# Differential attention layer: turning normalised tokens without TensorE, and 27 more exp blocks on VectorE

## What is computed

```python
h = _layernorm(x) * (1 + ca) + sa
q, k = einsum(h, Wq), einsum(h, Wk)          # 32 half-heads of 8 features; v: 16 heads of 16
attn_w = softmax(q @ k.T * hd ** -0.5)       # 2048 x 2048 for each half-head and batch
aw = attn_w[:, :, 0] - lam * attn_w[:, :, 1]
attn = rms_norm(aw @ v) * subln_w * (1 - LAMBDA_INIT)
x = x + ga * (attn @ Wo.T)
h = _layernorm(x) * (1 + cb) + sb
x = x + gb * (h @ (ternary(weight) * scale).T)
```

## Time and profile before

| | |
|---|---|
| median of 3 runs | 3611.5 us (3609.34 to 3612.31) |
| profiled execution | 3607.35 us, span 3605.5 us |
| granted TensorE clock, mean | 0.998 |
| PE busy | 3405.9 us, 94% |
| ScalarE busy | 3534.4 us, 98% |
| VectorE busy | 2588.9 us, 72% |
| GpSimd busy | 338.0 us, 9% |
| DMA | 136.90 MB, mean 38 GB/s |

### The profile page before, as it was taken

One profiled execution on the slowest core, in us unless ns is written; L12 is line 12 of the kernel. 1 busy time (PEld: TensorE's weight loads), 2 busy tenths in 40 slices (PEclk: granted clock), 3 DMA queues, 4 the chain that ended last, 5 costly groups with the idle time before them and its releaser, 6 DMA issues. The chain is left out here.

```text
span 3605.5 us, 76890 instructions
## 1 busy us (share of the span) xinstructions
PE 3405.9 (94%) x32302; PEld 799.1 (22%) x32302; DVE 2588.9 (72%) x3808; ACT 3534.4 (98%) x2808; POOL 338.0 (9%) x229
## 2 busy tenths in 40 slices
PE   8999999999899999999999999999999999989998
PEld 5222112122122222222222222222221222211222
DVE  6687878863578687776367768677547888878886
ACT  5999999999999999999999999999999999999998
POOL 3010101010010100101001010100100000000001
PEclk9999999999999999999999999999999999999999
DMA  6111110111101111101111001111012110010000
GB/s 196 28 32 39 32 31 22 35 39 33 38 21 42 48 35 40 50 23 33 36 47 50 25 31 36 40 49 36 20 31 63 45 37 22 17 30 16 20 22 26
DMA packets 103700, 136.90 MB, mean 38 GB/s; under 512 B 9916, under 2 KB 88716, under 8 KB 103340
## 3 DMA queue, kind: packets, MB, share of 16 engines
q1 hardware_dynamic: 102524, 131.01, 12.9%
q10 hardware_dynamic: 816, 0.79, 0.1%
HBM read 72.50 MB, written 59.19 MB: 37 GB/s over the span
## 5 line engine op out<-in xcount | busy, mean ns | idle before, releaser
L1146 ACT ACTIVATE probs<-ps 128x1536 f32<-128x1536 f32 (+1 forms) x2732 | 3497.4, 1670 | 15.5 <-PE ps L1263 13.9
L1291 PE MATMUL ps<-probs,values 128*32 128x512 f32 x14600 | 2047.9, 606 | 4.9 <-DVE wmod_sb L1644 2.4
L1263 PE MATMUL ps<-queries,keys 25*128 25x512 f16 x7680 | 1003.9, 385 | 160.6 <-ACT probs L1146 142.0
L1263 PEld LDWEIGHTS ps<-queries,keys 25*128 25x128 f16 x7680 | 249.8, 91 | 1947.3 <-ACT probs L1146 1861.5
L1291 PEld LDWEIGHTS ps<-probs,values 128*32 128x32 f32 x14600 | 300.2, 108 | 416.9 <-issue 410.5
L1623 DVE TENSOR_SCALAR d_y<-ps 128x512 f32<-128x512 f32 x240 | 165.6, 690 | 295.4 <-PE ps L1263 284.7
L1708 DVE STREAM_TRANSPOSE seg_t<-ps 128x512 f32<-128x512 f32 x127 | 91.0, 716 | 356.9 <-PE ps L1291 356.4
L1060 POOL TENSOR_TENSOR seg_rs<-seg_ms,neg_half 128x16 f32<-128x16 f32 x64 | 185.7, 2901 | 1506.1 <-DVE seg_ms L1721 1506.1
L1640 DVE SCALAR_TENSOR_TENSOR wmod_sb<-wmod_sb 128x1024 f32<-128x1024 f32 x204 | 249.6, 1224 | 6.3
L1644 DVE SCALAR_TENSOR_TENSOR wmod_sb<-wmod_sb,gates 128x1024 f32<-128x1024 f32 x204 | 249.5, 1223 | 6.0
L1642 DVE SCALAR_TENSOR_TENSOR wmod_sb<-wmod_sb,d_y 128x1024 f32<-128x1024 f32 x204 | 249.3, 1222 | 5.3
(11 more groups left out here) (181 smaller groups left out, 1690.9 us busy)
## 6 DMA issues: line engine op xcount, KB each, us to landing
v_scr<-a_v SPq DMA_DIRECT2D x16, 1024.0 KB, 5.6
values<-v_scr SPq DMA_DIRECT2D x29, 512.0 KB
queries<-q_scr SPq DMA_DIRECT2D x116, 96.0 KB
keys<-k_scr SPq DMA_DIRECT2D x116, 96.0 KB
e_x<-in_x_dram SPq DMA_DIRECT2D x18, 512.0 KB, 5.2
attn_scr<-seg_o SPq DMA_DIRECT2D x254, 32.0 KB
e_attn<-attn_scr SPq DMA_DIRECT2D x31, 256.0 KB, 3.6
out_dram<-e_y SPq DMA_DIRECT2D x15, 512.0 KB, 3.3
```

The costliest lines, as they stand in the source:

```text
L1146: nc.scalar.activation(probs[:, s % PRING, at, :], ps[:, base + at.start:base + at.stop:at.step, :], ACT.Exp, scale=1.0 / SQUARE).then_inc ...
L1263: last = nc.tensor.matmul(ps[:, score_bank(n), :], keys[buf][at, u * P:(u + 1) * P], queries[buf][at, tc * CH:(tc + 1) * CH], start=True, ...
L1291: last = nc.tensor.matmul(pv[row:row + VW, :], values[buf][:, n % SEG_BANKS // HEADS, j // 2, :], probs_of(n), start=(i == 0), stop=(i == ...
```

## The change

1. *Turning.* The transposes of `normed` leave PE, except for the first batch's prologue and the last 512 tokens. `norm_apply` writes `normed` ordered by squares; VectorE transposes the 32x32 squares in place of their grid (`turn_normed`, 1024 elements); SyncE moves the squares to their rows with 16 DMAs of 32 KB (`turn_squares`); GpSimd applies scale and shift (`scale_turned`, two instructions of 512 elements) and signals `a_evacuated` or `e_evacuated`. There are 27 turns: 12 of a-jobs and 15 of e-jobs. Steps 0 and 1 of a, 2 and 3 of e disappear from the schedule.
2. *Blocks.* `shared` gives two blocks to nearly every segment, 231 in all, at units 3 and 5, 8 and 10, with heads sought by `heads_of`; each block has its own scratch (`g_y`, `g_n`). `share_read` multiplies to 2^23 log2(e) and writes int32; whole and fractional part come out by bit operations, and three passes of polynomial and one product remain.
3. *Exp bias.* ScalarE's exp gets an immediate bias ln 8, to match the blocks' polynomial, which is scaled.
4. *Steps spread.* In the bodies of batches 1 and 2, except the last of each, the pieces stand every 2.8 units from unit 16 on.
5. *Short sums.* `segment_sums` is four entries: transpose and reciprocal at their place, the rest as filling work due three slots later. Norm statistics are due by slots after what they need, and GpSimd's order (`pool_order_of`) has its own clock and no wait for blocks.
6. In the prologue the first a-job's norm moves behind the gate weights.

```diff
-    D_UNITS = ((4, 6), (8, 10))
+    D_UNITS = ((3, 5), (8, 10))
     def shared(k):
...
-        return 2 if sum(light.get(step, 3) for step in steps) <= 5 and not normed else 1
+        return 2
...
+        if 0 < b < B - 1 and not turn:
+            spread = [[NB + 14 * (PIECES * j + p) // 5 for p in range(PIECES)] for j in range(A_MADE + len(E_MADE))]
+            put("a", body + NC, [(), ()] + spread[0:4] + spread[6:8])
+            put("e", body - GP, spread[4:6] + [(), ()] + spread[8:10])
...
+            if entry[0] == "sums":
+                later.extend((entry[2] + SUMS_AT, 0, SUMS_COST[part], ("rest", entry[1], part)) for part in range(1, sums_parts(entry[1])))
+            elif entry[0] in ("a_apply", "e_apply"):
+                later.append((slot_at(clock) + APPLY_AT, 0, 1600, ("turn", entry[0], entry[1])))
...
+            def turn_squares(kind, job):
+                sp.wait_ge(square_turned, TURN_OF[kind, job] + 1)
+                for row in range(P // 32):
+                    for col in range(P // 32):
+                        src = turned[32 * col:32 * col + 32, :, 32 * row:32 * row + 32]
+                        dst = hT[32 * row:32 * row + 32, :, :].rearrange("p c (n t) -> p (c n) t", n=BPC)[:, :, 32 * col:32 * col + 32]
+                        sp.dma_start(dst, src).then_inc(turn_done, DMA)
...
+            def scale_turned(kind, job, c):
+                if c == 0:
+                    pool.wait_ge(turn_done, (TURN_OF[kind, job] + 1) * SQUARES * DMA)
+                nc.gpsimd.tensor_scalar(hT[:, c, :], hT[:, c, :], cols_sb[:, first + 1, c, m:m + 1], cols_sb[:, first, c, m:m + 1], ALU.mult, ALU.add).then_inc(done, 1)
...
-                        if shares:
-                            pool.wait_ge(d_done, shares)
...
-                nc.scalar.activation(probs[:, s % PRING, at, :], ps[:, base + at.start:base + at.stop:at.step, :], ACT.Exp, scale=1.0 / SQUARE).then_inc(exp_done, 1)
+                nc.scalar.activation(probs[:, s % PRING, at, :], ps[:, base + at.start:base + at.stop:at.step, :], ACT.Exp, bias=EIGHT, scale=1.0 / SQUARE).then_inc(exp_done, 1)
...
-                            if i == 0 and p == 0:
-                                pe.wait_ge(a_normed, job + 1)
-                            elif i == 2 and p == 0:
+                            if i == A_FIRST_MADE and p == 0:
                                 pe.wait_ge(a_evacuated, (job - NC) * A_STEPS + 2)
...
+            def turn_normed(applied, job):
+                dve.wait_ge(a_normed if applied == "a_apply" else e_normed, job + 1)
+                dve.wait_ge(turn_done, TURN_OF[applied[0], job] * SQUARES * DMA)
+                V.transpose(turned[:, :, :].rearrange("p n f -> p (n f)"), normed[:, :, :].rearrange("p n e -> p (n e)")).then_inc(square_turned, 1)
...
                 if part == 0:
-                    link.then(V.tensor_scalar(d_n, y, ROUND, -ROUND, ALU.add, ALU.add))
+                    link.then(V.tensor_scalar(whole.bitcast(I32), f.bitcast(I32), WHOLE_BITS, WHOLE_FLIP, ALU.bitwise_and, ALU.bitwise_xor))
                 elif part == 1:
-                    link.then(V.scalar_tensor_tensor(d_y[:, :], d_n, SHIFT, y, ALU.subtract, ALU.subtract))
+                    link.then(V.tensor_scalar(f.bitcast(I32), f.bitcast(I32), PART_BITS, PART_SIGN, ALU.bitwise_and, ALU.bitwise_or))
                 elif part == 2:
-                    link.then(V.tensor_scalar(d_n.bitcast(mybir.dt.int32), d_n, BIAS, 2.0 ** 25, ALU.add, ALU.mult))
+                    link.then(V.scalar_tensor_tensor(f, f, POLY[0], f, ALU.add, ALU.mult))
```

More of the change, by code:

```diff
@@ L297, in schedule @@
                 opens = queue[0][0] == "m" or queue[0][3] == 0
-                if opens and s < closed + (NORMED if queue[0][0] == "e" and queue[0][2] == 2 else APART) and not last:
+                if opens and s < closed + APART and not last:
                     break
@@ L414, in order_of, with pool_order_of, first_of, take @@
         if b < B - 1:
-            order.append(("sums", (b + 1) * GP * SEGS - 1))
-        return order
+            k = (b + 1) * GP * SEGS - 1
+            order.append((clock, "sums", k, 0))
+            order.extend((clock, "rest", k, part) for part in range(1, sums_parts(k)))
+        return order
+    TURN_WAIT = 12000
+    def pool_order_of(b):
+        order, scales, held, clock = [], [], [], 0
+        def first_of(until):
+            heads = [queue for queue in (scales, held) if queue and max(clock, queue[0][0]) < until]
+            return min(heads, key=lambda queue: max(clock, queue[0][0])) if heads else None
+        def take(queue):
+            nonlocal clock
+            ready, cost, task = queue.pop(0)
+            order.append(task)
+            clock = max(clock, ready) + cost
+        for at, what, *task in order_of(b):
+            while first_of(at):
+                take(first_of(at))
+            if what == "turn":
+                scales.extend((at + TURN_WAIT, 800, ("scale", task[0][0], task[1], c)) for c in range(EC))
+            elif what in ("a_stats", "e_stats") or what == "rest" and task[1] == 3:
+                order.append((what, *task))
+                clock = max(clock, at) + (2900 if what == "rest" else 1010)
+            elif what == "evacuate" and task[0] == "a" and 2 <= task[2] < 6:
+                held.append((at, 1900, ("split", task[1], task[2] - 2)))
+        while first_of(STARTS[-1] + 10 ** 9):
+            take(first_of(STARTS[-1] + 10 ** 9))
+        return order
+    TURNS = [("a", NC)]
+    for body in range(B * GP):
+        for _, kind, job, i, p in sorted((u, *step) for u, step in steps_of(body).items()):
+            if kind == "e" and i == 1 and p == PIECES - 1:
+                TURNS.append(("e", job))
+        if body + 1 < (B - 1) * GP:
+            TURNS.append(("a", body + 1 + NC))
+    TURN_OF = {turn: n for n, turn in enumerate(TURNS)}
     LAST_JOB = (B - 1) * NC
@@ L1056, in _ @@
                         e_power(task[0])
-                    elif what == "sums" and (task[0] % 2 and task[0] < ALL_SEGS - 1 or task[0] == ALL_SEGS - 2):
+                    elif what == "rest":
                         rows = slice(0, P if task[0] % 2 else 64)
@@ L1897, in _ @@
                         a_apply(task[0])
+                    elif what == "turn":
+                        turn_normed(*task)
                     elif what == "gates":
```

258 lines of the change are left out of this document (135 added, 123 removed).

## The result

| | before | after |
|---|---|---|
| median | 3609.8 us (3608.48 to 3612.31, 6 runs) | 3596.8 us (3591.95 to 3600.04, 6 runs) |
| profiled execution | 3607.35 us, span 3605.5 | 3599.45 us, span 3597.6 |
| first exp | 76.1 us | 78.5 us |

The ratio is 0.996, 95% interval 0.9951 to 0.997: the change gains 13 us. The forecast was 3590, a gain of 21.5 on the median of 3611.5 known then; the time lies in its range of 3576 to 3608, and at the upper edge of its likeliest part, 3582 to 3597.

A forecast was written before the change was run, and what follows sets the result against it. ScalarE's exp stream was taken as the bound. Terms -22.7 - 4 - 6 + 9 + 2 = -21.7 took the profiled 3607.35 us to 3585.7, and the median, with its offset, to 3590; range 3576 to 3608.

The forecast's parts named there:

- Part 1, the slots: 27 more VectorE blocks turn 54 ScalarE exps from wide to narrow at 0.42 us each: -22.7 us.
- Part 2, PE's relief: Transposes leaving PE free 82 us of its work, little of it on the path: -4 us.
- Part 3, the turns hidden: The new chain VectorE, SyncE's DMAs, GpSimd's scales takes 13 to 16 us per turn and stays hidden: 0.
- Rival (c): Turns come late and PE's in-order queue holds scores and exps: +43 us at 24 us per turn, 3633; chance 0.07.
- Part 4, short sums: With only the reciprocal ahead of a segment's first read, stalls at twelve segment starts go: -6 us.
- Part 4, collisions: At seven places VectorE's evacuation, stats and the sums' rest between two reads delay scores by 1 to 1.7 us each: +9.
- the seven places: Spots where two VectorE reads stand around an evacuation, stats and the sums' rest, taking 5.6 us against three exps' 3.6.
- Part 5: GpSimd's splits and scales now run beside VectorE and lengthen its work, mostly off the path: +2 us.
- Bias 0 ns: The immediate bias in ScalarE's exps was taken to cost nothing: 0.
- contention: VectorE slowed by about 0.57 us per us of GpSimd, counting only just ahead of a read: +2 us.

The follow-up runs named there:

- e6: The changed kernel with the block pattern of the kernel before (27 segments have one block instead of two, 204 in all): 3617.6 us, ratio 1.0021 to the kernel before.
- e1: The changed kernel run again unaltered, beside the kernel before on the same chip: 3595.5 us, ratio 0.9958.
- e11: The kernel before with the changed kernel's 231 blocks, the rest of it kept: 3631.3 us, ratio 1.0057.
- e9: The changed kernel with each turn's 16 square DMAs cut in two (32 of 16 KB): 3678.9 us, ratio 1.0185 to the kernel before.
- e4: The kernel before with each segment's first block read at units 3 and 5 instead of 4 and 6: 3714.1 us, ratio 1.028.
- e7: The changed kernel with the rest of each segment's sums due at once, ahead of the first read: 3737.3 us, ratio 1.0352 to the kernel before.
- e3: The changed kernel with bounds and gates not allowed to run over VectorE's next due work: 3589.6 us, ratio 0.9938 to the kernel before.
- e5: The changed kernel with exp bias 0 instead of the immediate 2.079: 3598.9 us, ratio 0.9968 to the kernel before.
- e10: The changed kernel with the second pass of each of GpSimd's 48 splits done twice: 3598.1 us, ratio 0.9964 to the kernel before.
- e2: The changed kernel with reads in the first segments of batches 1 to 3 moved to units 5, 7, 9, 11: 3582.6 us, ratio 0.9924 to the kernel before.
- e8: The changed kernel with later first reads in batches 1 to 3, and bounds and gates kept off due work: 3575.3 us, ratio 0.9906 to the kernel before.

## Why the prediction was right, and where it was off

The sign, the range and the main mechanism, cheaper slots, were right; the account of what else the change costs was not, and errors in it partly cancelled. Of the 21.7 us forecast on the profiled execution, 7.9 came in the first trace of after and 12.8 in the second (spans 3605.5, 3597.6, 3592.7). The second balances so: slots -22.0, batch starts +4.9, other stalls at single places -1.1, first exp +2.9, many small delays +2.8, tail -0.4.

- **Part 1, the slots: right.** Two stretches of one piece each give the price. Before:

```profile
1983.64 733.75 ACT L1146 ACTIVATE probs<-ps 128x1536 f32<-128x1536 f32 x570 [0.15 <-PE ps L1263]
...
L1146 ACT ACTIVATE probs<-ps 128x1536 f32<-128x1536 f32 x494 | 692.7, 1759 | 0.3 <-PE ps L1263 0.2
L1146 ACT ACTIVATE probs<-ps 128x1024 f32<-128x1024 f32 x76 | 100.0, 1316 | 0.0
```

  After, the piece at 1051.09 above has 496 wide and 100 narrow in 758.61 us. The difference, 24.9 us for 2 wide and 24 narrow, gives 0.926 a narrow one with wide ones taken at 1.333: 0.407 per exp, 22.0 us for 54, where 22.7 was forecast. The medians of the distances between starts in the trace of after, 1.331 and 0.925, say the same. The bit passes took 0.69 as taken, VectorE's sum fell to 2566 (forecast 2550 to 2620), and e6 finds the 22 us again.
- **Part 2, PE's relief: not settled.** I took -4, and +2 for GpSimd beside VectorE. Nothing undid the relief alone, and no gain of this kind shows: delays of under 0.25 us between exps, where I had looked for it, add up to 13 us before and 16 in e1. PE's busy time fell by 49 us, not 82. In e11, with transposes on PE and 27 blocks more on VectorE, PE's queue waits for `normed` up to 4.7 us, 11.9 in three waits; so the relief's worth may depend on the blocks.
- **Part 3, the turns hidden: right, with luck.** The sum for a turn was 13 to 16 us; measured are 15.1 to 21.9 (issue 0.65 to 0.76 each, 11.72 for 16 in the turn shown under e9, not 0.46; scales 1.2 each on the mean, not 0.68). At the two tightest places the turn took 17.4 us, and I had the product 15 us behind its start: by my own cover it would have come 2.4 us late twice. It stood 17.8 behind and came 0.3 us behind the scale. Rival (c) took 43 us for turns of 24; no run has such turns, but e9's, of 25 to 31, cost 83, so its 43 was probably too low. Missing from it was the queue on GpSimd, which I had costed at nothing because the planner puts the scale 12 us behind the turn. That holds until a turn is late.
- **Part 4, short sums: here a term is missing, the move of the first reads.** "Twelve segment starts have a full sums entry ahead of a read. With reciprocal alone ahead of it I take -6": those stalls went for the most part (the piece of after that begins at 1051.09 runs through segment 36; away from the batch starts PE's waits for `d_y` fell from 6.2 us in 13 to 1.5 in 5, and waits for `g_y`, 3.1 us in 7, are new), but I priced the short sums against reads at unit 4 and did not price the move of all first reads to unit 3, which the diff holds. Without short sums the move costs the kernel before 103 us (e4), and leaving the short sums out of the changed kernel costs 141 (e7). With them it still costs the cover at three batch starts, 5 to 8 us more than before, and a good part of the missing gain went there. The row of before that should have warned is the one of d_y in the earlier trace rows (9.7 us of VectorE's idle time ended by "issue", in three waits): I left it out of the sum as small.
- **Part 4, collisions: +9 was too much.** Five of the seven places cost under 0.3 us and two about 0.5. From the first read to the second it took 3.5 to 4.8 us there, not 5.6. So the sign that I had named, waits of 1 to 1.7 us at these seven places and none elsewhere, did not come: the long waits for reads stood at the batch starts. What cost instead were the bounds ahead of seg_t at two other places, 5.9 us (e3), where I hadn't looked since no read stands between.
- **Part 5: right.** Bias 0 ns (e5), contention +2 taken and at most a few us found (e10, which adds to the splits alone); 0.33 us of VectorE per us of GpSimd in e10, not 0.57.

So the sum held by errors that partly cancel, which is luck: collisions 7 to 8 us too dear; not seen, 11 to 14 of batch starts and late transposes, 3 of a later first exp, and some 5 of small delays (3 more where 2 fewer were forecast). Together with the slots' 0.7 too little, and some 2 us more of the old stalls gone than forecast, these make, within their roundings, the 9 us by which the second trace missed the forecast; in the medians it is 7 (3597 against 3590).

What stays open: whether the prologue of after is later by itself (up to 2.5 us), what VectorE's pause at a batch's start is, and why it lasts 3.2 to 4.1 us in most traces and 5.7 and 5.8 at batch 1 in two (e7, after). A change in which the pause was removed, not covered, wasn't tried. Nor was the changed kernel with all its reads left at units 4 and 6: whether the move to 3 and 5 brings anything is not known.

## What to carry to other kernels

Price a moved instruction against what stands ahead of it in its new place, and parts of a change that lean on each other together: here 27 more blocks alone lose 20 us, reads one unit earlier alone 103, and the change without its short sums 141. A loss list grouped by place (where does the bound engine's timeline break?) found some 20 us in five places that the totals hid, and two small edits took it back. When a new chain goes through an in-order queue, look up not only who waits for it but what else is queued behind its wait.

## What the runs showed of the hardware

- A DMA between two places of the on-chip memory of 32 KB (32 partitions, runs of 128 B) cost SyncE 0.65 to 0.76 us to issue (16 in 11.72 us in the turn shown) and landed 2.0 us later; cut into halves, 32 of 16 KB took 21.47 us to issue, 0.67 each. Between these two sizes the price went by DMAs, not by bytes, and issue was most of a turn's 15 to 22 us.
- VectorE stood still for 3.2 to 5.8 us at the head of batches 1 to 3, with no releaser in the profile, in 12 of 14 traces; in the other two (e2, e8) its next read came late enough to hide it. Both kernels load a flag and branch there; that this is the cause is not shown.
- An immediate bias on the exp cost 0 ns. The Trainium skill (ScalarE: Activation LUTs, What ACT_TABLE_LOAD costs) says the same of immediates, and e5 agrees.
- After a pause of PE of 5.5 us (after) or 8 us (e9) the granted clock was 0.53 in the next 8 us and 0.57 in the next 5; after one of 2.0 us that ended at 1046.9 (after) it was 0.62 in the next 4, and another stall came too. A late read costs more than its wait.
